# One transformer block with routed experts on one core: engine orders and PSUM homes rewritten, a payload ring of 8, loads and empty rows spread over the loop

## The chip, the cores and the metric

The kernel runs on 1 core of one Trainium2 chip. The metric is the device time in microseconds of one execution. Engines are TensorE (PE), VectorE (DVE), ScalarE (ACT), GpSimd (POOL) and SyncE (SP, which issues most of the DMAs here).

## What is computed

The input x has 4 batches of 1024 tokens of 128 numbers, float32. Six vectors per batch come from a small matrix on silu(c) and shift, scale and gate the two halves of the block:

```python
h = _layernorm(x) * (1 + ca) + sa
x = x + ga * attention(h)          # 16 query heads, 4 key heads, D = 64
h = _layernorm(x) * (1 + cb) + sb
x = x + gb * moe(h)                # 8 experts, 128 -> 512 -> 128, relu
```

The attention is causal with a window of 128 tokens, and its scores go through 30 * tanh(s / 30) before the softmax. The expert of a token is the argmax of its gate logits. An expert takes at most 512 tokens, in the order of the tokens; the output of a token is scaled by its gate, and a token that found no place gets nothing from the experts.

## The kernel before, in words

A tile is 128 tokens (32 tiles, 8 per batch); a block is two tiles (16 blocks). Each engine has one program, an order written out by hand: a Python loop over e in steps of two, in which each call names the tile that it works on relative to e. All waiting is by semaphores, and each engine and the SP queue take their instructions strictly in order.

**Per block.** DVE takes the statistics of x (`measure1`, `gather1`), POOL makes 1/std (`rstd1_of`), ACT normalises (`normalise1`), PE turns the tile (`turn_x`, L348), ACT writes the high part XH with scale and shift (`high_x`), and DVE writes the full value into the bank and the low part XL (`full_x`, `low_x`). Products of float32 are made from a high and a low part in three passes. PE projects k, v and four groups of q (`project_k` L356, `project_v` L367, `project_q` L380), and ACT copies each result out of its bank (`keep_k`, `keep_v`, `keep_q`).

**Per tile and half of the heads.** `score` (L391) writes the scores against the own tile to the fixed PSUM tile `own` and those against the tile before to `turns`; since `own` is one buffer, a score waits for the tanh of the one before. DVE merges both (`merge`, L865), ACT takes tanh and exp (`weigh` L689, `expose` L695), and POOL masks (`mask`, L1177). `sums` (L477) and `attend` (L456, L463) follow. A query reaches back into the tile before, and for the second half of the queries attend reads VM, whose first 64 rows are V of the tile and whose last 64 are V of the tile before. SP mixes it by two DMAs (`mix_v`, L286), after `v_kept`, and `VM` is a ring of 4. DVE divides by the sums (`turn_sums`, `invert`, `spread`, `scale` L896), ACT takes the high part OH (L701) and POOL the low part OL (`low_o`, L1185). `out_project` (L482) makes 24 matmuls per block, with OH and OL in turn.

**Then per tile.** ACT scales by ga (`keep_y`, L711), PE turns back (`turn_y`), DVE adds x (`add_x`, L907) and normalises again (`normalise2`, `modulate2`, `shift2`, the last of them frees the bank of `turn_y`), PE turns h (`turn_h2`) and scores the experts (`score_experts`), DVE finds the largest (`top8`, `which`), POOL marks it and counts (`mark`, `add_seen`), PE counts the places (`count`), DVE reads the place (`locate`), and POOL scatters the row PAY, which has h, the gate row, x and the token's number, to its place in `sorted_rows` in DRAM (`scatter`, L1221). SP also stores x to the output (`store_x`, L291). PAY is a ring of 4 rows of 400 numbers.

**Banks.** `turns` has six PSUM banks. The table HOME says which bank each use takes, and `take` waits for the engine that frees the bank's last use.

**Head.** SP loads x of batch 0, c, wmod, wk, wv, wq, the other three batches, wo, Wg and b1 (L253 to L263), then writes the empty rows for all 8 experts (L266, from the last row of PAY), then handles the small mod table, then w1 in one load of 2 MB (L276), and only then enters its loop with the `mix_v` of tile 1.

**Experts.** After the loop SP waits for all scatters and loads each expert's 512 rows and its w2 (L310 to L319). PE turns the rows (L596), makes the up and down products (L604, L617), ACT takes relu, DVE finishes, and POOL scatters to the output.

Of the kernel before, what the change touches and what calls it, by code (L numbers as in the profile page):

```python
# [37 lines left out]
ROW_H, ROW_G, ROW_X, ROW_ID, ROW = 0, P, 2 * P, 3 * P, 400  # L38
NO_TOKEN = 1 << 20

K_RING, Q_RING, V_RING, VD_RING, VM_RING, P_RING, PAY_RING = 3, 2, 6, 4, 4, 4, 4
# [5 lines left out]
    ("columns",): 0, ("rows",): 1,  # L47
    ("before", 0, 0): 2, ("before", 0, 1): 2, ("before", 1, 0): 2, ("before", 1, 1): 1,
    ("count", 0): 2, ("count", 1): 1,
    ("h2", 0): 4, ("h2", 1): 4,  # L50
    ("k",): 4,
    ("logits", 0): 4, ("logits", 1): 2,
    ("pv", 0): 4, ("pv", 1): 4,
    ("q", 0): 4, ("q", 1): 5, ("q", 2): 5, ("q", 3): 3,
    ("sums", 0): 5, ("sums", 1): 0,
    ("v",): 1,
    ("wo",): 1,
    ("x",): 1,
    ("y", 0): 1, ("y", 1): 0,
# [26 lines left out]
def build(nc, x, wq, wk, wv, wo, wg, w1, b1, w2, b2, c, wmod, out):  # L86
# [3 lines left out]
    with ctx:  # L90
# [28 lines left out]
        rows_at = sb("rows_at", [P, 2 * ST * ROW])  # L119
# [46 lines left out]
        empty_row = PAY[:, PAY_RING - 1, :]  # L166
# [3 lines left out]
        for wide in (rows_at[:, :], x_sb[:, :, :].rearrange("p a b -> p (a b)"),  # L170
                     Q[:, :, :, :].rearrange("p a b c -> p (a b c)"), PR[:, :, :].rearrange("p a b -> p (a b)")):
            for i in range(wide.shape[1] // (ST * ROW)):
                rows.append(wide[:, i * ST * ROW:(i + 1) * ST * ROW].rearrange("p (s r) -> p s r", r=ROW))
# [13 lines left out]

        x_in = [sem(f"x_in{b}") for b in range(BATCHES)]
        wk_in, wv_in, wq_in, c_in, wmod_in, wo_in, w1_in, b2_in, rest_in, mod_in = sems(
            "wk_in", "wv_in", "wq_in", "c_in", "wmod_in", "wo_in", "w1_in", "b2_in", "rest_in", "mod_in")  # L190
# [44 lines left out]
            (WkH[:, :], WkL[:, :], stage_k), (WqH[:, :QH], WqL[:, :QH], stage_q[:, :QH]), (WvH[:, :], WvL[:, :], stage_v),  # L235
            (WqH[:, QH:], WqL[:, QH:], stage_q[:, QH:]),
            (WoH[:, REP:, :], WoL[:, REP:, :], stage_o[:, REP:, :]), (WoH[:, :REP, :], WoL[:, :REP, :], stage_o[:, :REP, :]))
        SPLIT_K, SPLIT_Q0, SPLIT_V, SPLIT_Q1, SPLIT_O1, SPLIT_O0 = range(6)
        split_in = (wk_in, wq_in, wv_in, wq_in, wo_in, wo_in)
        CONSTS = 14  # L240
# [8 lines left out]
        def program_sp(sp):  # L249
# [3 lines left out]
            sp.dma_start(x_sb[:, 0:BATCH_TILES, :], x_v[0]).then_inc(x_in[0], 16)  # L253
            sp.dma_start(cT[:, :], c).then_inc(c_in, 16)
            sp.dma_start(stage_m, wmod).then_inc(wmod_in, 16)
            sp.dma_start(stage_k, wk).then_inc(wk_in, 16)
            sp.dma_start(stage_v, wv).then_inc(wv_in, 16)
            sp.dma_start(stage_q, wq).then_inc(wq_in, 16)
            for b in range(1, BATCHES):
                sp.dma_start(x_sb[:, b * BATCH_TILES:(b + 1) * BATCH_TILES, :], x_v[b]).then_inc(x_in[b], 16)  # L260
# [3 lines left out]
            sp.wait_ge(consts, CONSTS)  # L264
            for e in range(EXPERTS):
                sp.dma_start(sorted_v[e], empty_row.unsqueeze(1).to_broadcast([P, ST, ROW])).then_inc(empty_in, 16)  # L266
# [6 lines left out]
            sp.wait_ge(weights_l, len(split))  # L273
            sp.wait_ge(columns_done, 1)
            sp.wait_ge(rows_done, 1)
            sp.dma_start(w1_sb, w1.rearrange("e h f -> h e f")).then_inc(w1_in, 16)  # L276
# [16 lines left out]
            for e in range(-24, TILES - 14, 2):  # L293
                if is_tile(e + 23):
                    mix_v(e + 23)
                if is_tile(e + 14):
                    store_x(e + 14)
                if is_tile(e + 15):
                    store_x(e + 15)
                if is_tile(e + 24):  # L300
                    mix_v(e + 24)
# [21 lines left out]
        def program_pe(pe):  # L323
# [158 lines left out]
            def out_project(k):  # L482
                n, ps = take("wo", k)
                if k == 0:
                    pe.wait_ge(weights_l, SPLIT_O0 + 1)
                pe.wait_ge(ol_done, 4 * k + 4)
                y = ps[:, 0:BT]
                for i in range(2 * REP):
                    oh, ol = (o[:, :, :, i * HALF:(i + 1) * HALF] for o in (OH, OL))
                    pe.matmul(y, WoH[:, i, :], oh, start=(i == 0), stop=False)  # L490
                    pe.matmul(y, WoH[:, i, :], ol, start=False, stop=False)  # L491
                    last = pe.matmul(y, WoL[:, i, :], oh, start=False, stop=(i == 2 * REP - 1))  # L492
                last.then_inc(wo_done, 1)
                freed[n] = yT_kept, k + 1
# [37 lines left out]
            n, ps = take("rows")  # L532
            pe.matmul(ps[0:BATCHES, 0:3 * P], siluT[:, :], stage_m[:, 3 * P:6 * P], start=True, stop=True).then_inc(rows_done, 1)
# [5 lines left out]
            for e in range(-20, TILES - 8, 2):  # L539
                if is_tile(e + 10):  # L540
                    turn_h2(e + 10)
                if is_tile(e + 16):
                    project_q(e // 2 + 8, 1)
                    project_q(e // 2 + 8, 0)
                    project_q(e // 2 + 8, 3)
                if is_tile(e + 9):
                    count(e + 9)
                if is_tile(e + 14):
                    sums(e + 14)
                if is_tile(e + 10):  # L550
                    score_experts(e + 10)
                if is_tile(e + 15):
                    score(e + 15, 1)
                if is_tile(e + 14):
                    attend(e + 14)
                if is_tile(e + 16):
                    project_v(e // 2 + 8)
                    score(e + 16, 0)
                if is_tile(e + 12):
                    out_project(e // 2 + 6)  # L560
                if is_tile(e + 10):
                    count(e + 10)
                if is_tile(e + 11):
                    turn_h2(e + 11)
                if is_tile(e + 18):
                    project_q(e // 2 + 9, 2)
                if is_tile(e + 12):
                    turn_y(e + 12)
                if is_tile(e + 11):
                    score_experts(e + 11)  # L570
                if is_tile(e + 15):
                    sums(e + 15)
                if is_tile(e + 18):
                    project_k(e // 2 + 9)
                if is_tile(e + 16):
                    score(e + 16, 1)
                if is_tile(e + 15):
                    attend(e + 15)
                if is_tile(e + 20):
                    turn_x(e // 2 + 10)  # L580
                if is_tile(e + 17):
                    score(e + 17, 0)
                if is_tile(e + 13):
                    turn_y(e + 13)
# [47 lines left out]
        def program_act(act):  # L632
# [86 lines left out]
            def gate_row(t):  # L719
                act.wait_ge(gate_done, t + 1)  # L720
                if t == 0:
                    act.wait_ge(mod_in, 16)
                    act.wait_ge(empty_in, 16 * EXPERTS)
# [11 lines left out]

            act.wait_ge(c_in, 16)
            act.activation(c_e[:, :], cT[:, :], ACT.Exp, scale=-1.0).then_inc(c_exped, 1)
            split_high(SPLIT_K)
            split_high(SPLIT_Q0)
            split_high(SPLIT_V)  # L740
            split_high(SPLIT_Q1)
# [3 lines left out]
            for e in range(-18, TILES - 4, 2):  # L745
                if is_tile(e + 10):
                    expose(e + 10, 1)
                if is_tile(e + 9):
                    high_o(e + 9, 0)
                if is_tile(e + 6):  # L750
                    keep_h2(e + 6)
                if is_tile(e + 14):
                    high_x(e // 2 + 7)
                if is_tile(e + 12):
                    keep_q(e // 2 + 6, 1)
                if is_tile(e + 11):
                    weigh(e + 11, 0)
                if is_tile(e + 12):
                    keep_q(e // 2 + 6, 0)
                if is_tile(e + 11):  # L760
                    expose(e + 11, 0)
                if is_tile(e + 12):
                    keep_q(e // 2 + 6, 3)
                if is_tile(e + 9):
                    high_o(e + 9, 1)
                if is_tile(e + 11):
                    weigh(e + 11, 1)
                if is_tile(e + 5):
                    gate_row(e + 5)
                if e == -12:  # L770
                    split_high(SPLIT_O1)
                    split_high(SPLIT_O0)
                if is_tile(e + 12):
                    keep_v(e // 2 + 6)
                if is_tile(e + 6):
                    exp_gate(e + 6)
                if is_tile(e + 11):
                    expose(e + 11, 1)
# [531 lines left out]
```

## Time and profile before

| | |
|---|---|
| median of 3 runs | 476.62 us (475.41 to 477.88) |
| the profiled execution | 476.81 us, its span 475.1 us |
| mean granted clock of TensorE | 0.952 |
| busy: PE, POOL, ACT, DVE | 88%, 65%, 63%, 60% of the span |
| head, up to the first projection | 0 to 13.3 us |
| loop over the tiles | 13.3 to some 397 us |
| experts | 397 to 475 us |

A row of the timeline has the start and length in us, engine, line, operation, output <- inputs and count; what stands in brackets is the idle time before it and what ended it. A matmul's length includes its way through the array, so that those of one group overlap; the distance of two starts says more than the length. In the page and the windows "PEclk" is the granted clock as a share of full speed, where 0.50 is 1.2 GHz and 1.00 is 2.4 GHz.

### The profile page before, as it was taken

To read this page: it belongs to the slowest core of one execution; us is meant where nothing else is said; L and a number is where in the kernel's file an instruction comes from. 1 tells how busy PE (TensorE), PEld (TensorE's weight loads), DVE (VectorE), ACT (ScalarE), POOL (GpSimd) and SP (SyncE) were. 2 spreads that over 40 slices of the span, in tenths; PEclk is the share of its full clock that TensorE was granted. 3 is DMA by queue.
4 is the path that set the end of the run, shared out by engine and by line. 5 is a ranking of instruction groups with operands and counts; after the bars stand their busy time and mean duration, and the time that the engine had idled before them with its cause. 6 is when DMAs were issued, how large, how long until landed. Compare 5 with 4: busy or idle time off the path is not lost. (4 is left out here: it accounts for less than half of the span.)

```text
span 475.1 us, 14910 instructions
## 1 busy us (share of the span) xinstructions
PE 417.4 (88%) x5608; PEld 294.0 (62%) x5608; DVE 286.9 (60%) x846; ACT 298.0 (63%) x537; POOL 310.8 (65%) x494
## 2 busy tenths in 40 slices
PE   2894999999999999999999999999999742899970
PEld 1652566766767676666677666767565531799960
DVE  6263557775676868576777756675777541245631
ACT  4785457777776868777777778676756221564420
POOL 6136248587786969687867878676769851055572
PEclk9998899999999999999999999999999765999995
DMA  8987000101101010102011110101020125971110
GB/s 261 369 294 231 3 23 3 41 25 37 52 20 54 20 52 20 43 19 70 20 52 38 35 41 21 52 20 52 21 86 24 42 96 188 364 248 39 33 50 16
DMA packets 32078, 37.73 MB, mean 79 GB/s; under 512 B 3474, under 2 KB 28311, under 8 KB 32008
## 3 DMA queue, kind: packets, MB, share of 16 engines
q1 hardware_dynamic: 28936, 28.22, 19.1%
q0 software_dynamic: 3072, 8.56, 5.0%
q8 instruction: 46, 0.75, 0.6%
q14 instruction: 24, 0.20, 0.1%
HBM read 15.88 MB, written 17.31 MB: 70 GB/s over the span
## 5 line engine op out<-in xcount | busy, mean ns | idle before, releaser
L1185 POOL TENSOR_TENSOR OL<-O,OH 128x512 fp32r<-128x512 f32 x64 | 81.3, 1285 | 22.3 <-ACT OH L701 21.8
L865 DVE COPY_PREDICATED own<-before,turns 128x1024 f32<-128x1024 uint32 x56 | 68.8, 1229 | 40.3 <-PE turns L424 40.3
L689 ACT ACTIVATE PR<-own 128x1024 f32<-128x1024 f32 x64 | 65.5, 1024 | 42.4 <-DVE own L865 42.0
L1177 POOL TENSOR_SCALAR_AFFINE_SELECT PM<-PR 128x1024 f32<-128x1024 f32 x64 | 69.5, 1096 | 22.4 <-ACT PR L695 22.0
L695 ACT ACTIVATE PR<-PR 128x1024 f32<-128x1024 f32 x64 | 65.8, 1054 | 0.0
L420 PE MATMUL own<-Q,K 64*32 64x256 f32 (+3 forms) x896 | 58.8, 441 | 1.9 <-ACT PR L689 1.7
L896 DVE TENSOR_TENSOR O<-turns,R 128x512 f32<-128x512 f32 x64 | 41.2, 685 | 29.2 <-PE turns L463 28.9
L424 PE MATMUL turns<-Q,K 64*32 64x128 f32 (+3 forms) x896 | 57.4, 429 | 0.0
L701 ACT ACTIVATE OH<-O 128x512 fp32r<-128x512 f32 x64 | 40.0, 628 | 11.0 <-DVE O L896 10.9
L1221 POOL DMA_INDIRECT sorted_rows<-PAY,slot_i x32 | 35.1, 1096 | 14.0 <-issue 10.9
L424 PEld LDWEIGHTS turns<-Q,K 64*32 64x32 f32 x896 | 36.5, 107 | 9.4
L456 PE MATMUL turns<-PR,V 128*32 128x256 f32 x448 | 36.4, 394 | 6.1 <-DMA VM<-V 6.1
L344 PE MATMUL turns<-XH,WqH 128*128 128x256 f32 x128 | 39.2, 307 | 2.0 <-DVE XL L859 1.8
L675 ACT ACTIVATE Q<-turns 128x512 f32<-128x512 f32 x64 | 38.5, 601 | 4.0 <-PE turns L346 3.8
L490 PE MATMUL turns<-OH,WoH 128*128 128x256 f32 x128 | 38.4, 300 | 2.0 <-POOL OL L1185 2.0
L491 PE MATMUL turns<-OL,WoH 128*128 128x256 f32 x128 | 36.7, 287 | 0.0
L492 PE MATMUL turns<-OH,WoL 128*128 128x256 f32 x128 | 36.7, 286 | 0.0
L345 PE MATMUL turns<-XL,WqH 128*128 128x256 f32 x128 | 36.0, 281 | 0.0
L346 PE MATMUL turns<-XH,WqL 128*128 128x256 f32 x128 | 35.9, 280 | 0.0
L456 PE MATMUL turns<-PR,VM 128*32 128x256 f32 x448 | 35.8, 388 | 0.0
L463 PE MATMUL turns<-PM,VD 64*32 64x256 f32 x896 | 31.7, 391 | 0.0
L874 DVE STREAM_TRANSPOSE sumsT<-turns 128x512 f32<-128x512 f32 x32 | 22.9, 716 | 13.0 <-PE turns L477 12.2
(189 smaller groups left out, 1010.8 us busy)
## 6 DMA issues: line engine op xcount, KB each, us to landing
sorted_rows<-PAY SPq DMA_DIRECT2D x8, 800.0 KB, 12.1
VM<-V SPq DMA_DIRECT2D x56, 64.0 KB, 2.1
x_sb<-x_dram SPq DMA_DIRECT2D x4, 512.0 KB, 6.7
w_stage<-w_dram SPq DMA_DIRECT2D x1, 2048.0 KB, 10.9
out_dram<-PAY SPq DMA_DIRECT2D x32, 64.0 KB, 1.7
x_sb<-sorted_rows SPq DMA_DIRECT2D x2, 800.0 KB, 9.6
Q<-sorted_rows SPq DMA_DIRECT2D x2, 800.0 KB, 9.1
PR<-sorted_rows SPq DMA_DIRECT2D x2, 800.0 KB
```

The lines of the kernel that those rows point to most:

```text
L344: pe.matmul(dst, wh, xh, start=True, stop=False)
L420: pe.matmul(own[lo:lo + B, a, :].rearrange("p (r n) -> p r n", n=P)[:, :, lo:P], keys(a, t, lo, lo + B), q(a, lo, P), start=True, stop=Tru ...
L424: last = pe.matmul(ps[lo:lo + B, a, :].rearrange("p (r n) -> p r n", n=P)[:, :, 0:lo + B], keys(a, t - 1, lo, lo + B), q(a, 0, lo + B), st ...
L456: last = pe.matmul(out_of(c, x, g), v[:, d], probabilities(PM if first(t) else PR, slice(0, P), g, c), start=(x == 0), stop=(x == 1 and fi ...
L675: act.activation(Q[:, k % Q_RING, 2 * n:2 * n + 2, :], bank["q", k, n].rearrange("p (c n) -> p c n", c=2), ACT.Copy).then_inc(q_kept[n], 1)
L689: act.activation(pr, own[:, :, :].rearrange("p a n -> p (a n)"), ACT.Tanh, scale=SCORE_SCALE).then_inc(tanhed, 1)
L695: act.activation(pr, pr, ACT.Exp, scale=SOFTCAP).then_inc(exped, 1)
L701: act.activation(OH[:, t % 2, c, :], O[:, t % 2, c, :], ACT.Copy).then_inc(oh_done, 1)
L865: dve.copy_predicated(own[:, :, :].rearrange("p a (r n) -> p (a r) n", n=P), before[:, :].bitcast(U32).unsqueeze(1).to_broadcast([P, 2 * R ...
L896: dve.tensor_tensor(O[:, t % 2, c, :].rearrange("p (x r n) -> p x r n", x=2, n=HALF), bank["pv", t][:, c, :].rearrange("p (x r n) -> p x r ...
L1177: pool.affine_select(out=PM[:, u % P_RING, :].rearrange("p (r n) -> p r n", n=P), in_=PR[:, u % P_RING, :].rearrange("p (r n) -> p r n", n ...
L1185: pool.tensor_tensor(OL[:, t % 2, c, :], O[:, t % 2, c, :], OH[:, t % 2, c, :].bitcast(F32), ALU.subtract).then_inc(ol_done, 1)
```

## The change

- A row of PAY has 388 numbers instead of 400, in another order (h, number, gate, x), and PAY is a ring of 8. The empty row is a buffer of its own; scatter(0) alone waits for the empty rows, no longer `add_x`, `gate_row` and `name_row`.
- SP loads x of the first two tiles alone, then wk, wq in two parts, wv, the rest of batch 0, batch 1, wo, Wg, b1. ACT's queue loads c and wmod in two parts. The empty rows of two experts each stand behind the `mix_v` of tiles 1 to 4, batches 2 and 3 behind those of tiles 5 and 6, and w1 goes expert by expert behind later `store_x`.
- The splits into high and low parts have another order, and the copies for ga are made later (`keep_gate`).
- `out_project` makes the 16 matmuls with OH first, then waits for OL and makes its 8.
- All five engine orders and the table HOME are new. In PE's, V and one group of q are projected at the start of an iteration, before the attend of the tile two before them.
- The expert rows are read to other buffers (rows_at, Q, PR, x_sb, OH).

The orders of ACT, DVE and POOL are cut to the calls that matter below; the places of the others have moved too.

```diff
-K_RING, Q_RING, V_RING, VD_RING, VM_RING, P_RING, PAY_RING = 3, 2, 6, 4, 4, 4, 4
+K_RING, Q_RING, V_RING, VD_RING, VM_RING, P_RING, PAY_RING = 3, 2, 6, 4, 4, 4, 8
 HOME = {
...
+    ("before", 0, 0): 3, ("before", 0, 1): 1, ("before", 1, 0): 0, ("before", 1, 1): 3,
+    ("count", 0): 2, ("count", 1): 0,
+    ("h2", 0): 2, ("h2", 1): 1,
+    ("k",): 1,
+    ("logits", 0): 3, ("logits", 1): 2,
+    ("pv", 0): 1, ("pv", 1): 3,
+    ("q", 0): 3, ("q", 1): 5, ("q", 2): 5, ("q", 3): 2,
+    ("sums", 0): 1, ("sums", 1): 5,
+    ("v",): 4,
+    ("wo",): 4,
+    ("x",): 0,
+    ("y", 0): 0, ("y", 1): 5,
...
         def program_sp(sp):
+            sp.dma_start(x_sb[:, 0:2, :], x_v[0][:, 0:2, :]).then_inc(x_first, 16)
             sp.dma_start(stage_k, wk).then_inc(wk_in, 16)
+            sp.dma_start(stage_q[:, QH:], wq[:, QH:]).then_inc(wq1_in, 16)
+            sp.dma_start(stage_q[:, :QH], wq[:, :QH]).then_inc(wq0_in, 16)
             sp.dma_start(stage_v, wv).then_inc(wv_in, 16)
+            sp.dma_start(x_sb[:, 2:BATCH_TILES, :], x_v[0][:, 2:BATCH_TILES, :]).then_inc(x_in[0], 16)
+            sp.dma_start(x_sb[:, BATCH_TILES:2 * BATCH_TILES, :], x_v[1]).then_inc(x_in[1], 16)
...
-            for e in range(EXPERTS):
-                sp.dma_start(sorted_v[e], empty_row.unsqueeze(1).to_broadcast([P, ST, ROW])).then_inc(empty_in, 16)
...
-            sp.dma_start(w1_sb, w1.rearrange("e h f -> h e f")).then_inc(w1_in, 16)
...
+            for e in range(14, TILES + 22, 2):
+                if is_tile(e - 15):
+                    mix_v(e - 15)
+                if 1 <= e - 15 <= EXPERTS // 2:
+                    clear_rows(2 * (e - 15) - 2)
+                    clear_rows(2 * (e - 15) - 1)
+                if EXPERTS // 2 < e - 15 <= EXPERTS // 2 + 2:
+                    load_x(e - 15 - EXPERTS // 2 + 1)
+                if is_tile(e - 14):
+                    mix_v(e - 14)
+                if 1 <= e - 14 <= EXPERTS // 2:
+                    clear_rows(2 * (e - 14) - 2)
+                    clear_rows(2 * (e - 14) - 1)
...
+                if is_tile(e - 21):
+                    store_x(e - 21)
+                if is_tile(e - 20):
+                    store_x(e - 20)
+                if W1_TILE <= e - 22 < W1_TILE + 2 * EXPERTS:
+                    load_w1((e - 22 - W1_TILE) // 2)
...
             def out_project(k):
+                pe.wait_ge(oh_done, 4 * k + 4)
+                for i in range(2 * REP):
+                    oh = OH[:, :, :, i * HALF:(i + 1) * HALF]
+                    pe.matmul(y, WoH[:, i, :], oh, start=(i == 0), stop=False)
+                    pe.matmul(y, WoL[:, i, :], oh, start=False, stop=False)
                 pe.wait_ge(ol_done, 4 * k + 4)
                 for i in range(2 * REP):
+                    last = pe.matmul(y, WoH[:, i, :], OL[:, :, :, i * HALF:(i + 1) * HALF], start=False, stop=(i == 2 * REP - 1))
...
```

PE's new order in one iteration, each call under its own `is_tile`:

```python
for e in range(-16, TILES - 4, 2):
    project_v(e // 2 + 6); score_experts(e + 6); project_q(e // 2 + 6, 3); count(e + 5)
    sums(e + 10); turn_x(e // 2 + 8); score(e + 11, 1); attend(e + 10)
    out_project(e // 2 + 4); project_q(e // 2 + 7, 1); count(e + 6); turn_h2(e + 7)
    score(e + 12, 0); project_k(e // 2 + 7); turn_y(e + 8); score_experts(e + 7)
    sums(e + 11); project_q(e // 2 + 7, 0); score(e + 12, 1); attend(e + 11)
    project_q(e // 2 + 7, 2); score(e + 13, 0); turn_y(e + 9); turn_h2(e + 8)
```

Of DVE's (range(-8, TILES + 12, 2)), at e == 0 and then in each iteration:

```python
    measure1(e + 6)
    if e == 0: keep_columns(); split_low(SPLIT_K); split_low(SPLIT_Q1)
    full_x(e // 2); merge(e - 5, 1); spread(e - 6)
    if e == 6: split_low(SPLIT_O1); split_low(SPLIT_O0)
    ...
    merge(e - 4, 1); normalise2(e - 8); invert(e - 5); modulate2(e - 8); spread(e - 5)
    shift2(e - 8); scale(e - 5, 0); gather1(e + 7); scale(e - 5, 1); merge(e - 3, 0)
```

Of ACT's (range(-16, TILES - 2, 2)):

```python
    expose(e + 7, 1); keep_y(e // 2 + 2); keep_h2(e + 3); keep_q(e // 2 + 5, 1); gate_row(e + 2)
    keep_k(e // 2 + 5); weigh(e + 8, 0)
    ...
```

## Rows read from the trace of the kernel before

**Rows 1.** Page, part 1 (busy us, share, instructions); part 2, granted clock in 40 slices

```profile
PE 417.4 (88%) x5608; PEld 294.0 (62%) x5608; DVE 286.9 (60%) x846; ACT 298.0 (63%) x537; POOL 310.8 (65%) x494
...
PEclk9998899999999999999999999999999765999995
```

**Rows 2.** Windows: stretch, length, busy us by engine, granted clock, DMA share, GB/s

```profile
13.30:39.60 26.30, 24.74 (x280) 17.43 (x280) 11.45 (x24) 20.49 (x33) 8.41 (x15) 1.00 0.95 327
39.60:45.60 6.00, 0.00 (x0) 0.01 (x1) 2.47 (x5) 3.25 (x4) 5.01 (x5) 0.88 0.85 259
45.60:51.10 5.50, 5.48 (x65) 2.25 (x65) 0.00 (x0) 0.00 (x0) 0.21 (x1) 0.51 0.01 3
51.10:371.70 320.60, 316.32 (x4830) 212.86 (x4822) 224.05 (x661) 233.04 (x421) 240.35 (x380) 1.00 0.12 36
371.70:376.20 4.50, 1.12 (x9) 0.68 (x6) 2.71 (x13) 2.00 (x6) 4.50 (x7) 0.90 0.08 28
376.20:381.50 5.30, 5.26 (x24) 5.20 (x25) 1.00 (x3) 0.00 (x0) 2.83 (x9) 0.50 0.10 39
```

**Rows 3.** PE's waits, whole span: us in total, times, longest

```profile
PE turns L456 <- DMA VM<-V: 6.1, 1, 6.1
```

**Rows 4.** Timeline of the SP queue, 0 to 60 us: start, length, issues

```profile
10.76 11.56 SPq L266 DMA_DIRECT2D sorted_rows<-PAY  x8
...
34.20 0.38 SPq L276 DMA_DIRECT2D w_stage<-w_dram  x1
```

**Rows 5.** Page, part 6, whole span; last line: tile VM, 30 to 60 us

```profile
sorted_rows<-PAY SPq DMA_DIRECT2D x8, 800.0 KB, 12.1
...
VM<-V SPq DMA_DIRECT2D x56, 64.0 KB, 2.1
...
DMA to landing us min/median/max: 6.8/8.5/10.2
```

**Rows 6.** Timeline of PE: attend of a later tile, up to the next group

```profile
199.64 0.64 PE L456 MATMUL turns<-PR,V 128*32 128x256 f32 x8
...
202.53 0.44 PE L352 MATMUL turns<-ident,XN 128*128 128x128 f32 x2
```

**Rows 7.** Timeline of the head: first statistics, landing of wq, first projection

```profile
5.85 0.48 DVE L845 BATCH_NORM_STATS2 stats<-x_sb 128x6 f32<-128x128 f32 x2
...
8.07 0.63 ACT L635 ACTIVATE WqH<-w_stage 128x512 fp32r<-128x512 f32 x1 [1.28 <-DMA w_stage<-wq_dram]
...
13.30 0.55 PE L344 MATMUL turns<-XH,WqH 128*128 128x256 f32 x1 [1.83 <-DVE XL L859]
```

**Rows 8.** Timeline of PE: turn_x, one per block, of three blocks

```profile
51.08 0.44 PE L352 MATMUL turns<-ident,XN 128*128 128x128 f32 x2
...
72.26 0.44 PE L352 MATMUL turns<-ident,XN 128*128 128x128 f32 x2
...
312.49 0.44 PE L352 MATMUL turns<-ident,XN 128*128 128x128 f32 x2 [0.38 <-DVE PAY L933]
```

**Rows 9.** Page, part 5: the merge and the tanh between two scores

```profile
L865 DVE COPY_PREDICATED own<-before,turns 128x1024 f32<-128x1024 uint32 x56 | 68.8, 1229 | 40.3 <-PE turns L424 40.3
...
L689 ACT ACTIVATE PR<-own 128x1024 f32<-128x1024 f32 x64 | 65.5, 1024 | 42.4 <-DVE own L865 42.0
```

**Rows 10.** Timeline of PE: out_project at full clock, and what follows it

```profile
214.27 0.39 PE L490 MATMUL turns<-OH,WoH 128*128 128x256 f32 x1
...
217.12 0.18 PE L519 MATMUL turns<-onehot,earlier_b 128*128 128x8 bf16 x1
```

**Rows 11.** Timeline of the last block and its out_project

```profile
359.53 0.65 PE L420 MATMUL own<-Q,K 64*32 64x512 f32 x12 [0.67 <-ACT PR L689]
...
373.21 0.62 ACT L701 ACTIVATE OH<-O 128x512 fp32r<-128x512 f32 x1
...
373.62 2.47 POOL L1185 TENSOR_TENSOR OL<-O,OH 128x512 fp32r<-128x512 f32 x2
...
376.24 0.55 PE L490 MATMUL turns<-OH,WoH 128*128 128x256 f32 x1 [2.02 <-POOL OL L1185]
```

More of the change, by code:

```diff
@@ L46 @@
 HOME = {
[L47 to L59, printed above, removed]
+    ("columns",): 4, ("rows",): 2,
+    ("before", 0, 0): 3, ("before", 0, 1): 1, ("before", 1, 0): 0, ("before", 1, 1): 3,
[10 more added lines that the diff above has]
+    ("y", 0): 0, ("y", 1): 5,
 }
@@ L556, in program_pe @@
[L556 to L582, printed above, removed]
@@ L583, in program_pe @@
-                if is_tile(e + 13):
-                    turn_y(e + 13)
+                    turn_x(e // 2 + 8)
+                if is_tile(e + 11):
+                    score(e + 11, 1)
+                if is_tile(e + 10):
+                    attend(e + 10)
+                if is_tile(e + 8):
+                    out_project(e // 2 + 4)
+                if is_tile(e + 14):
+                    project_q(e // 2 + 7, 1)
+                if is_tile(e + 6):
+                    count(e + 6)
+                if is_tile(e + 7):
+                    turn_h2(e + 7)
@@ L587, in program_pe @@
+                if is_tile(e + 11):
+                    attend(e + 11)
+                if is_tile(e + 14):
+                    project_q(e // 2 + 7, 2)
+                if is_tile(e + 13):
+                    score(e + 13, 0)
+                if is_tile(e + 9):
+                    turn_y(e + 9)
+                if is_tile(e + 8):
+                    turn_h2(e + 8)
             for n in range(6):
@@ L841, in measure1 @@
             def measure1(t):
[L842 removed]
+                dve.wait_ge(x_first if t < 2 else x_in[t // BATCH_TILES], 16)
                 if t >= 2:
@@ L1048, in program_dve @@
[L1048 to L1057 removed]
+                if is_tile(e - 6):
+                    scale(e - 6, 0)
+                if is_tile(e - 9):
+                    modulate2(e - 9)
+                    shift2(e - 9)
@@ new lines, in program_dve @@
+                if is_tile(e - 8):
+                    normalise2(e - 8)
+                if is_tile(e - 5):
+                    invert(e - 5)
+                if is_tile(e - 8):
+                    modulate2(e - 8)
+                if is_tile(e - 5):
+                    spread(e - 5)
+                if is_tile(e - 8):
+                    shift2(e - 8)
+                if is_tile(e - 5):
+                    scale(e - 5, 0)
+                if is_tile(e + 7):
+                    gather1(e + 7)
```

472 lines of the change are left out of this document (236 added, 236 removed).

## The prediction

> **What bounds the kernel now.** The profiled execution took 476.81 us for a span of 475.1; the median of the three runs is 476.62, so the two can be used as one. All sums below are against 476.81. A measurement of this kernel can tell about 0.5% (2.4 us) from no change.
>
> I read the page first. PE is busy 88% and the next engine 65%, and the granted clock is below full in the slices around 48 us, from 368 to 416 us, and at the end [rows 1]. So I cut the span into windows at the places where PE stops [rows 2]. The long loop, 51.1 to 371.7, has 316.3 us of PE in 320.6. Its busy number is modelled, so I checked it by starts: turn_x runs once per block of two tiles, and from 51.08 to 312.49 it starts 13 times, 12 blocks of 21.78 us on average, the shortest 21.18 [rows 8]. A new order can win at most 12 x 0.60 = 7.2 us there. The losses of PE stand elsewhere. From 39.6 to 45.6 it does nothing, and then works until 51.1 at half clock (0.51) [rows 2]. The wait list names the cause: attend of tile 1 waits 6.1 us for the mixed V in VM [rows 3]. The SP timeline shows what these transfers stand behind: eight issues of empty rows from 10.76 that take 11.56 us, then the 2 MB of w1 at 34.20, and the VM transfers behind both [rows 4]. The first six take 6.8 to 10.2 us to land, where the median over the run is 2.1 [rows 5]. At the end, out_project of the last block waits until 376.24 for POOL's low parts and then runs at half clock until 381.5 [rows 2, 11].
>
> **The mixed V no longer waits (gain 8.6).** In the new SP program the VM transfers of tile 1 stand before any empty row, and w1 comes in eight pieces much later. V is also projected one block earlier against attend (project_v of tiles e+12, e+13 before attend of e+10), so the transfer has over a tile's time. The clears of two experts stand between the transfers of tiles 2 and 3: some 1.6 MB, which at 327 GB/s [rows 2] are 4.9 us, and tile 3's attend comes a tile later, half a block or 10.6 us [rows 8]. The 6.0 us of standstill go. The attend after it took 5.5 us; one at full clock takes 202.53 - 199.64 = 2.9 [rows 6], so the clock gives back 2.6. Sum 8.6. If the cover is gone (clears landing late), at most these 8.6 come back.
>
> **Head (gain 0).** x of tiles 0 and 1 comes alone and c and wmod go by ACT's queue. But DVE's new list has the statistics of tiles 2 to 6 before keep_columns, the splits and full_x(0), and those tiles sit behind x_first, wk, wq, wv. The bytes up to the end of batch 0 are the same 1.6 MB that had landed before when wq was there, at 8.07 [rows 7]. Behind it come three pairs of statistics at 0.5 to 0.7 each [rows 7], two splits, full_x and low_x, again near 13 us: first projection 13.2 against 13.30 [rows 7]. If DVE does not wait there, up to 2 us are won; if x arrives later, 1 is lost.
> A sentence on the queue by itself: the Trainium skill (DMA: Bandwidth & Descriptors, Issuing engines are not separate DMA queues) says that DMAs started by different engines share the same 16 DMA engines and only the issue time is saved. This speaks against a gain from ACT's queue and no run here shows it yet; the sum takes none either way.
>
> **Ramp (gain 0, from -3 to +2).** Before, 13.3 to 39.6 is 26.3 us with 24.7 of PE [rows 2]. The scores go one by one through own: a score needs the tanh of the one before, thus merge 1.23 and tanh 1.02 plus the latencies between [rows 9]. The new order does turn_x, q, k of the next block between them, also V and q3 of this one, but ACT has keep_k(1) before the first tanh, and DVE has the two splits of Wo (2 x 0.6) in the block of scores 1 and 2. I count three gaps of about 1 us for the new, for 1.6 us that the old one has idle and some that are hidden in its half-clock start. It is no row: I take 0 and keep both ends.
>
> **Loop (loss 1.5, from -5 to +1).** The same matmuls in another order; out_project has the same 24. All PSUM homes move. Two new meetings are tight: bank 4 holds y of out_project and the second half of the next score's before, with only q1, count and turn_h2 between; bank 0 is held by y of a tile until shift2, which DVE now does after merge 1.23, normalise2, invert, modulate2 and spread, while score(e+13, 0) wants bank 0 after attend 2.9 and q2. By durations the two come out within 0.5 us of each other. I put 0.1 us on each of 14 blocks. 0.35 each is the bad end; of the possible 7.2 gain I allow 1.
> The ring of 8 payloads removes waits of DVE and POOL only, which are not the bound: 0. The cover is PE's full loop. The rows of 388 numbers instead of 400 take 3% off transfers of the expert stage that run ahead of PE there: 0.
>
> **Last block (loss 1.3, from 0 to -2).** Before, the old order has out_project between score(30, 0) and score(30, 1). The new one has projections there, which do not exist for the last block; what is left is a turn_y, an expert score and sums, about 1.5 us, against merge and tanh with latencies, about 2.6. This costs 1.1, and the next score pair, which waits 0.67 now [rows 11], a little more.
>
> **Last out_project (gain 3.5, from 2.5 to 4.9).** It used to start when OL was there (373.62 + 2.47 = 376.09, start 376.24). Sixteen of its 24 matmuls now need OH alone, done at 373.83 [rows 11]. At full clock 24 take 2.85 us (217.12 - 214.27) [rows 10], so 16 from 373.9 end at 375.8, and 8 with OL, ready at about 375.7, end at 376.7. Against 381.5 this gives 4.8. If the clock is half from the start, as it was at 376.2 [rows 2], 16 take 3.5 and 8 take 1.8: 379.2, gain 2.3. The clock was still 0.90 over 371.7 to 376.2, so it lies between; I take 3.5. What comes behind it (YT, the norms, routing, the scatter, the load of rows) is the same chain and moves with it.
>
> **Sum.** 8.6 + 0 + 0 - 1.5 - 1.3 + 3.5 = 9.3 us, 476.81 - 9.3 = 467.5.
>
> **Rivals.**
> A. The forecast, 467.5: chance 0.61.
> B. The loop has room. For it: the loop's weight loads are busy 212.9 of 320.6 us, 66% [rows 2]. Against: blocks already repeat within 0.6 us of the shortest. If the new order took 5 of the 7.2 us instead of losing 1.5, the time is 461.0. Chance 0.14. By the Trainium skill (Trainium Kernel Development and Optimization, Best Practices) matmul busy time misleads and LDWEIGHTS busy share tells the distance to the roofline; by that rule there is a third of the loop free, and B would be too small. The trace speaks against it: the spacing of the 24 matmuls at full clock is 0.119 us each, without a wait.
> C. The stall moves. A mixed V of tile 3 or 5 lands behind the clears beside it, or the ramp loses what the stall had hidden: PE waits, and the clock falls again. Price: the 8.6 gone, thus 476.1. For it: VM landings of up to 10.2 us behind other transfers [rows 5]. Against: over a tile of slack. Chance 0.13.
> D. Slower. DVE's shift2 comes too late for score(e+13, 0) by bank 0 in every block. One us per block over 14 blocks, instead of 1.5 in all, makes 467.5 + 12.5 = 480.0. Without its 1.5 the loop would leave 466.0, so it passes the old time from 0.76 us per block (466.0 + 10.6). For it: merge and the five operations behind it fill the gap to within 0.5 us. Against: DVE is busy 224 of 320.6 us. Chance 0.12.
>
> **Numbers.** Bounds of A: best 476.81 - (8.6 + 2 + 2 + 1 + 4.9) = 458.3, worst 476.81 - (8.6 - 1 - 3 - 5 - 2 + 2.5) = 476.7; all ends together are unlikely. 461 to 474.5 leaves out half of C, most of D and little of A and B, together under 0.2. Faster by over 0.5% (below 474.2): A 0.59, B 0.14, C 0.05, D 0.04, sum 0.82. Within 0.5%: A 0.02, C 0.06, D 0.02, sum 0.10. Slower: C 0.02, D 0.06, sum 0.08.
>
> **What would show it.** No wait of PE for VM, and no half clock before 60 us, shows the first step. The first projection near 13 and the first turn_x after attend(1) some 8 us earlier show head and ramp. The distance of turn_x over twelve blocks shows the loop: 261 to 263 for A, under 257 for B, over 268 for D, with the wait named at scores or project_v. OH matmuls at least 2 us before the last OL end shows the last step. It would be wrong if VM waits return, if the loop grows, or if PE's pause in the last block is longer than 3 us.

## The result and the profile after

The changed kernel takes 465.13 us (median of 4, 464.12 to 465.36) against 476.09 for the kernel before beside it: ratio 0.976, 95% interval 0.9728 to 0.9792, 11.0 us. Measured again later beside the kernel before, it gave 465.17 and 0.9764 (0.9734 to 0.9794). The forecast was 467.5 in a range of 461 to 474.5. The profiled execution took 464.12 us, 12.7 less than that of before; 1.4 of these belong to the last stretch, from the last down product to the end, which took 16.4 us in this trace, 17.8 before and 18.0 in the second trace of the changed kernel.

The page after, busy time and granted clock, answers to [rows 1]:

```profile
PE 413.0 (89%) x5608; PEld 291.8 (63%) x5608; DVE 285.5 (62%) x846; ACT 299.7 (65%) x537; POOL 309.5 (67%) x495
...
PEclk9999999999999999999999999999999955999996
```

The dip of the clock in the fourth and fifth slices is gone. The windows of the changed kernel (stretch, length, busy us by engine PE, PEld, DVE, ACT, POOL, then granted clock, DMA share, GB/s), cut at the first projection, the end of attend(1), the end of the last attend, and around the last out_project, answer to [rows 2]:

```profile
14.10:44.83 30.73, 29.04 (x352) 20.46 (x351) 16.60 (x42) 24.66 (x39) 12.70 (x21) 1.00 0.57 196
44.83:362.80 317.97, 314.94 (x4821) 211.77 (x4813) 221.56 (x658) 233.43 (x419) 241.14 (x379) 1.00 0.17 50
362.80:365.70 2.90, 0.91 (x15) 0.59 (x7) 2.05 (x7) 1.67 (x4) 2.65 (x4) 1.00 0.18 69
365.70:369.30 3.60, 3.11 (x24) 2.92 (x25) 1.23 (x9) 1.06 (x4) 3.34 (x8) 1.00 0.06 18
```

The 6 us without PE and the attend at half clock have no counterpart. The last out_project runs at full clock in this trace. In the second trace of the same kernel it does not: there the window around it has

```profile
364.20:368.80 4.60, 4.60 (x27) 4.56 (x27) 1.51 (x9) 0.61 (x3) 3.89 (x9) 0.63 0.05 14
```

The waits of PE in the changed kernel, first trace, answer to [rows 3]:

```profile
PE turns L375 <- ACT XN L671: 5.5, 1, 5.5
...
PE turns L544 <- POOL onehot L1237: 3.8, 3, 2.1
PE turns L530 <- DVE PAY L965: 3.2, 3, 2.5
...
PE own L443 <- ACT PR L718: 2.0, 3, 1.4
```

No wait for VM is left. On the SP queue of the changed kernel (start, length, issue), the VM transfers stand ahead of the empty rows, as against [rows 4]:

```profile
22.13 1.17 SPq L297 DMA_DIRECT2D VM<-V  x2
23.35 1.16 SPq L279 DMA_DIRECT2D sorted_rows<-empty_row  x2
...
30.72 1.11 SPq L297 DMA_DIRECT2D VM<-V  x2
31.87 1.17 SPq L279 DMA_DIRECT2D sorted_rows<-empty_row  x2
33.08 2.63 SPq L297 DMA_DIRECT2D VM<-V  x2
```

By the view of tile VM from 15 to 60 us they land in 1.9 to 5.9 us, where it was 6.8 to 10.2 [rows 5]:

```profile
DMA to landing us min/median/max: 1.9/2.0/5.9
```

**Where the time went.** I put the traces side by side at places where PE has done the same work. The second trace of the changed kernel was taken later; its time, 465.33 us, is the nearer to the median.

| place | before | after | second trace after | lead of after | lead of second |
|---|---|---|---|---|---|
| first projection | 13.30 | 14.10 | 13.68 | -0.8 | -0.4 |
| end of attend(1), 1.3 us of work (a turn_x, a group of q) more done in after | 51.08 | 44.83 | 43.35 | 7.5 | 9.0 |
| end of the last attend | 371.68 | 362.82 | 361.33 | 8.9 | 10.3 |
| YT of the last block | 381.74 | 368.84 | 368.84 | 12.9 | 12.9 |
| first rows of the experts turned | 400.13 | 388.30 | 387.57 | 11.8 | 12.6 |
| start of the last down product | 457.23 | 445.87 | 445.62 | 11.4 | 11.6 |
| end of the span | 475.1 | 462.3 | 463.6 | 12.8 | 11.5 |

### The profile page after: what moved, and what is told of

Read it like the earlier page. It is cut to its first block and busy times, and to the rows that moved or that the text cites. A ratio compares the mean times of both kernels' runs of the same rounds, so it can differ in the third digit from the quotient of the medians.

```text
span 462.3 us, 14917 instructions
## 1 busy us (share of the span) xinstructions
PE 413.0 (89%) x5608; PEld 291.8 (63%) x5608; DVE 285.5 (62%) x846; ACT 299.7 (65%) x537; POOL 309.5 (67%) x495
## 5 line engine op out<-in xcount | busy, mean ns | idle before, releaser
L724 ACT ACTIVATE PR<-PR 128x1024 f32<-128x1024 f32 x64 | 67.1, 1048 | 0.1
L443 PE MATMUL own<-Q,K 64*32 64x128 f32 (+3 forms) x896 | 58.7, 441 | 2.5 <-ACT PR L718 2.0
L930 DVE TENSOR_TENSOR O<-turns,R 128x512 f32<-128x512 f32 x64 | 43.0, 682 | 17.2 <-PE turns L486 17.0
L1262 POOL DMA_INDIRECT sorted_rows<-PAY,slot_i x32 | 34.7, 1085 | 12.3 <-issue 11.5
L447 PEld LDWEIGHTS turns<-Q,K 64*32 64x32 f32 x896 | 36.6, 107 | 9.5
L367 PE MATMUL turns<-XH,WqH 128*128 128x256 f32 x128 | 41.1, 321 | 0.0
L367 PEld LDWEIGHTS turns<-XH,WqH 128*128 128x128 f32 x128 | 25.0, 195 | 18.7 <-issue 9.5
L479 PE MATMUL turns<-PR,V 128*32 128x256 f32 x448 | 35.1, 385 | 0.0
L479 PE MATMUL turns<-PR,VM 128*32 128x256 f32 x448 | 34.4, 379 | 0.0
L513 PE MATMUL turns<-OH,WoH 128*128 128x256 f32 x128 | 32.7, 294 | 0.9 <-ACT OH L730 0.9
L1231 POOL TENSOR_SCALAR var<-mv 128x1 f32<-128x1 f32 x32 | 6.2, 192 | 38.8 <-DVE mv L949 37.5
L514 PE MATMUL turns<-OH,WoL 128*128 128x256 f32 x128 | 31.0, 281 | 0.0
```

The lines of the kernel that those rows point to most:

```text
L367: pe.matmul(dst, wh, xh, start=True, stop=False)
L443: pe.matmul(own[lo:lo + B, a, :].rearrange("p (r n) -> p r n", n=P)[:, :, lo:P], keys(a, t, lo, lo + B), q(a, lo, P), start=True, stop=Tru ...
L447: last = pe.matmul(ps[lo:lo + B, a, :].rearrange("p (r n) -> p r n", n=P)[:, :, 0:lo + B], keys(a, t - 1, lo, lo + B), q(a, 0, lo + B), st ...
L479: last = pe.matmul(out_of(c, x, g), v[:, d], probabilities(PM if first(t) else PR, slice(0, P), g, c), start=(x == 0), stop=(x == 1 and fi ...
L724: act.activation(pr, pr, ACT.Exp, scale=SOFTCAP).then_inc(exped, 1)
L930: dve.tensor_tensor(O[:, t % 2, c, :].rearrange("p (x r n) -> p x r n", x=2, n=HALF), bank["pv", t][:, c, :].rearrange("p (x r n) -> p x r ...
```

## The experiments

**1. Which load made the stall: w1 alone.** The prediction blamed both the empty rows and w1. The first edit moves only w1 in the kernel before, with the three waits ahead of it, one of them for the splits of Wo:

```diff
-            sp.dma_start(w1_sb, w1.rearrange("e h f -> h e f")).then_inc(w1_in, 16)
+                if e + 14 == 8:
...
+                    sp.dma_start(w1_sb, w1.rearrange("e h f -> h e f")).then_inc(w1_in, 16)
```

> The kernel before, with one edit: the 2 MB load of w1 moves from ahead of the first mixed V to behind the store of tile 9. Theory (the stall is the w1 load): the first VM transfers are issued at 33.3 instead of 34.63 and have only the 768 KB mod load ahead, land by 38.5, before attend of tile 1 is ready at 39.5; the 6.0 us of standstill and the 2.6 us of half clock go, 476.1 - 8.6 = 467.5. Rival (the empty rows are the cause, since SP reaches its loop only at 32.9 behind them): VM still lands late, gain under 3 us, 473 or more.

Measured: 469.08 us against 475.87, ratio 0.9848 (0.9829 to 0.9868), a gain of 6.8. The timeline and, in the last line, the view of tile VM up to 60 us:

```profile
33.00 0.35 SPq L271 DMA_DIRECT2D mod<-mod_dram  x1
33.40 2.70 SPq L281 DMA_DIRECT2D VM<-V  x3
...
43.53 0.44 PE L352 MATMUL turns<-ident,XN 128*128 128x128 f32 x2
...
DMA to landing us min/median/max: 1.9/2.2/4.0
```

VM is issued hardly earlier (33.4 instead of 34.6), but it lands in 4.0 us at most, and turn_x of block 3, at 51.08 before, comes at 43.53. The rival falls. The gain is 1.8 short of the forecast. Some 1.0 of it is there at turn_x of block 3, since attend(1) is not ready at 39.5 here but starts at 40.64, of which 0.6 us is a later first projection (13.89). The lead is still 7.7 when the first rows of the experts are turned (392.39 against 400.13), and 6.5 at the start of the last down product; why 1.2 us go there stays open.

**2. The empty rows alone.**

```diff
-            for e in range(EXPERTS):
-                sp.dma_start(sorted_v[e], empty_row.unsqueeze(1).to_broadcast([P, ST, ROW])).then_inc(empty_in, 16)
...
+                if 1 <= t <= EXPERTS // 2:
+                    for e in (2 * t - 2, 2 * t - 1):
+                        sp.dma_start(sorted_v[e], empty_row[:, :].unsqueeze(1).to_broadcast([P, ST, ROW])).then_inc(empty_in, 16)
```

> The kernel before, with the empty rows of two experts each behind the mixed V of tiles 1 to 4 (an empty row buffer of its own, scatter(0) alone waits for them), w1 still in one load ahead of the loop. Theory: SP waits there for the splits of Wo, which DVE ends at 34.2, so w1 and the VM transfers behind it start no earlier than before, and the stall stays: 474 to 477. Rival (empty rows are the cause): 467.5.

Measured: 475.01, ratio 0.9973 (0.9957 to 0.9988), 0.9 us. PE's wait list first, then the SP timeline, of this kernel:

```profile
PE turns L462 <- DMA VM<-V: 5.0, 1, 5.0
```

```profile
15.08 0.35 SPq L268 DMA_DIRECT2D mod<-mod_dram  x1
35.19 0.38 SPq L273 DMA_DIRECT2D w_stage<-w_dram  x1
35.61 0.60 SPq L283 DMA_DIRECT2D VM<-V  x1
```

SP issues nothing from 15.4 to 35.2: it stands at its wait for the last split of Wo, which DVE ends at 35.16, and the VM transfers stand behind that wait and behind 2 MB. The stall stays, as expected. In the kernel before the same wait held SP for 0.9 us only (the mod table's load was issued at 32.93, behind the empty rows, and w1 at 34.20). So either of the two, the empty rows or the wait, puts w1 at this time, and this run alone does not say that the empty rows were harmless; run 1 does, where they and the mod table stay in front.

**3. Both.** The two edits together.

> The kernel before, with both edits: empty rows behind the mixed V of tiles 1 to 4 and w1 behind the store of tile 9. Theory: the stall goes as with w1 alone, 467.5, at most 1 us from that run. Rival (each of the two carries a part): at least 3 us below the better of the two single edits.

Measured: 468.33, ratio 0.9833 (0.9815 to 0.9852). That is 7.5 us of gain, 0.75 below w1 alone, with overlapping intervals. The VM transfers of tile 1 are issued at 23.0 now, ten us earlier than in run 1, and it hardly matters. The loads account for 7.5 of the 11.0 us, almost all by w1.

**4. The old SP order in the changed kernel.** Empty rows and w1 ahead of the loop again:

```diff
+            for e in range(EXPERTS):
+                sp.dma_start(sorted_v[e], empty_row[:, :].unsqueeze(1).to_broadcast([P, ST, ROW])).then_inc(empty_in, 16)
...
+            sp.dma_start(w1_sb, w1.rearrange("e h f -> h e f")).then_inc(w1_in, 16)
```

> The changed kernel, with empty rows and w1 put back ahead of SP's loop, all else as changed. Theory: w1 is issued near 34.5 again and VM of tile 1 lands near 45, where attend of tile 1 is ready at 41.9: 3 to 4 us of standstill and 1 to 2.6 us of half clock, 465.1 + 5 = 470. Rival (the new order needs the early VM more, tiles 2 and 3 wait too): over 473. Rival (the new order would have hidden it anyway): 465 to 466.

Measured: 472.64 (470.08 to 474.8), ratio 0.9932 (0.9907 to 0.9958). PE's wait list and the SP timeline:

```profile
PE turns L466 <- DMA VM<-V: 4.5, 1, 4.5
```

```profile
35.59 0.38 SPq L282 DMA_DIRECT2D w_stage<-w_dram  x1
36.01 3.94 SPq L292 DMA_DIRECT2D VM<-V  x6
```

The stall is back at the same place, with VM issued within 1.4 us of the old time. The profiled execution, 470.08, is the theory's 470; the median is 2.6 above, and its executions scatter more than those of the other kernels. By the ratios the old SP order costs 8.2 us here (0.9932 against 0.976). The rival that the new order hides the stall is out. The rival of over 473 is not: three of the seven executions took 473.5 to 474.8, and what makes them slower stays open, since only the fastest was profiled.

**5. The old out_project in the changed kernel.**

```diff
+                pe.wait_ge(ol_done, 4 * k + 4)
...
-                pe.wait_ge(oh_done, 4 * k + 4)
...
-                    pe.matmul(y, WoL[:, i, :], oh, start=False, stop=False)
-                pe.wait_ge(ol_done, 4 * k + 4)
...
+                    pe.matmul(y, WoH[:, i, :], ol, start=False, stop=False)
+                    last = pe.matmul(y, WoL[:, i, :], oh, start=False, stop=(i == 2 * REP - 1))
```

> The changed kernel, with the old out_project (OH and OL passes in turn, one wait for OL ahead). Theory: the last one starts when OL is there, 1.9 us later (367.6 instead of 365.7) or more, and perhaps at half clock, which costs 2 to 4 us; the other 15 give back 0.10 us each (2.85 us in the trace before, 2.95 after), 1.5 us. Net 465.1 + 1.5, between 465.5 and 468. Rival (OL is ready in time in the new order anyway): 463.6, since only the 1.5 us remain.

Measured: 467.0 against 465.13 to 465.17 of the changed kernel, ratio 0.981 (0.9791 to 0.983). Its last out_project in the timeline:

```profile
366.64 0.55 PE L513 MATMUL turns<-OH,WoH 128*128 128x256 f32 x1 [2.88 <-POOL OL L1224]
...
371.04 0.47 ACT L738 ACTIVATE YT<-turns,ga_col 128x256 f32<-128x256 f32 x1 [5.56 <-PE turns L515]
```

It waits 2.88 us for OL, and its first matmul has the length of half clock (0.55); the mean granted clock of the product, 366.64 to 371.01, is 0.68. The kernel of run 6 differs from this one in block 15 alone and took 464.54 beside it, so the split in the last block is worth 2.5 us.

**6. Is the new pass order dearer per block?** Out_project takes 2.94 to 2.96 us per block in the trace after and 2.84 to 2.94 before. I held the pass order responsible and kept it for block 15 alone:

```diff
+                if k == BLOCKS - 1:
+                    ...
+                else:
+                    ...
```

> The changed kernel, with the old out_project in blocks 0 to 14 and the new one in block 15 alone. Theory (the new pass order costs 0.10 us per block by its matmuls): 465.1 - 1.5 = 463.6. Rival (the 0.10 us lies in how the trace counts a group's end, or is taken back at the next group): 465.1.

Measured: 464.54, ratio 0.9754 (0.9735 to 0.9773), 0.6 us below the changed kernel, within its interval and between the two expectations, so the time decides nothing. The trace does: blocks 0 to 14 still take 2.94 to 2.96 us, with the old pass order. The 0.1 us is not the pass order; I was wrong. What else in the new order makes it was not tried.

**7. The new out_project alone, in the kernel before.** The edit is the one of the change.

> The kernel before, with the new out_project alone. Theory: in the last block 16 matmuls run before OL is there and the clock stays up, 3.3 us gained, less 15 times 0.10: 476.1 - 1.8 = 474.3. Rival (the clock falls there anyway): 476.1 - 2.3 + 1.5 = 475.3. Rival (a part of the changed loop's gain comes from it): below 473.

Measured: 474.16 against 476.35, ratio 0.9951 (0.9934 to 0.9968), a gain of 2.2. The theory said 474.3, but with a cost of 1.5 us in the loop that does not exist (blocks of 2.83 to 2.94 us here, as before); the agreement is luck, and the gain at the end is smaller than the 3.3 that it took. In this trace the way from the last attend to YT is 7.1 us instead of 10.1. The timeline shows why it is not shorter:

```profile
373.72 0.28 PE L491 MATMUL turns<-OH,WoL 128*128 128x256 f32 x1
373.83 0.28 PE L490 MATMUL turns<-OH,WoH 128*128 128x256 f32 x1
373.94 0.34 PE L491 MATMUL turns<-OH,WoL 128*128 128x256 f32 x1
374.08 0.42 PE L490 MATMUL turns<-OH,WoH 128*128 128x256 f32 x1
374.30 0.42 PE L491 MATMUL turns<-OH,WoL 128*128 128x256 f32 x1
```

The distance of two starts grows from 0.11 to 0.22 us in the middle of the product: the clock had stayed up through the start and fell to half during it. In the first trace of the changed kernel it stayed at 1.00 to the end, in the second it fell after six matmuls, at 365.0.

**8. The ring of 8.**

```diff
-K_RING, Q_RING, V_RING, VD_RING, VM_RING, P_RING, PAY_RING = 3, 2, 6, 4, 4, 4, 8
+K_RING, Q_RING, V_RING, VD_RING, VM_RING, P_RING, PAY_RING = 3, 2, 6, 4, 4, 4, 4
```

> The changed kernel with a payload ring of 4 instead of 8. Theory (the ring takes away only waits of engines with slack): 465.1, within 1 us. Rival (the new SP order stores x of tile t only after the mixed V of tile t + 6 or t + 7, so DVE's add_x waits and holds the merge behind it): 2 us or more slower, with PE waits at scores.

Measured: 464.34, ratio 0.9752 (0.9732 to 0.9772). The ring of 8 brings nothing, as the prediction had it, and the blocks of this trace repeat as those of the changed kernel do.

**9. A better head.** DVE of the changed kernel stands still until x of tiles 2 to 7 is there, with the work of tile 0 behind it. The edit puts that work first:

```diff
+                if e == -4:
+                    keep_columns(); split_low(SPLIT_K); split_low(SPLIT_Q1); full_x(0); low_x(0)
+                if e == -2:
+                    split_low(SPLIT_Q0); split_low(SPLIT_V)
...
-                if is_tile(e + 16):
+                if is_tile(e + 16) and e != -14:
                     turn_x(e // 2 + 8)
...
                     project_q(e // 2 + 7, 0)
+                if e == -14:
+                    turn_x(1)
```

> The changed kernel with DVE's head in another order: keep_columns, splits of K and Q1, full_x(0), low_x(0) stand before the statistics of tiles 2 and 3, the splits of Q0 and V before those of 4 and 5; turn_x(1) goes behind the projection of q group 0. Theory (the head waits for x of tiles 2 to 7, which lands at 9.25): the first projection starts near 10 instead of 14.1, and of the 4 us some 2 to 4 reach the end: 461 to 463. Rival (ACT and DVE chains of the ramp decide, not PE's start): the scores come as late as before, 464.5 to 465.5.

Measured: 461.36, but beside a kernel before that took 471.17 on that chip, ratio 0.9804 (0.9788 to 0.982). The absolute time looks like a success, and the ratio, 9.8 us of gain where the changed kernel had 11.0, says that there is none. The head did move, by its timeline:

```profile
11.25 0.58 PE L367 MATMUL turns<-XH,WqH 128*128 128x256 f32 x1 [2.89 <-DVE WqL L875]
...
15.09 0.38 PE L375 MATMUL turns<-ident,XN 128*128 128x128 f32 x2
```

The first projection comes at 11.25, not near 10, since it now waits for the split of q. From there to turn_x of block 4 it is 36.6 us, and 35.5 and 34.4 in the two traces of the changed kernel: the chain of scores, tanh and merge in the ramp takes part or all of the gain back.

**10. Head and last block together,** then both kernels once more on one chip.

> Both: the head as above, and the new out_project in block 15 alone. Theory: the two gains add, 1.5 us below the head alone. Rival: within 0.5 us of the head alone.

Measured: 460.65, ratio 0.9775 (0.9761 to 0.979), 0.7 below the head alone. That lies between theory and rival and decides nothing.

> The changed kernel again, beside the next. Theory: the same ratio to the kernel before as the first time, 0.976, whatever chip it falls on. The stretch from the last down product's start to the end, 16.4 us in its first trace and 17.7 to 17.9 in those of seven other kernels, is 17.7 or so again if it is a matter of the execution, 16.4 if it is one of this kernel.

Measured: 465.17, ratio 0.9764 (0.9734 to 0.9794). First projection 13.68, turn_x of block 4 at 48.08. The last stretch took 18.0 us, so the 16.4 of the first trace was a matter of the execution. So was more: turn_x of block 4 came at 49.57 there, and the last out_project ran at full clock there and fell to half clock here.

> The changed kernel with DVE's new head and the new out_project in the last block alone. Theory (half a microsecond from each): 0.5 to 1.5 us below the changed kernel on the same chip. Rival (the ramp takes the head's gain back): within 0.5 us of it.

Measured: 465.37, ratio 0.9775 (0.9746 to 0.9803), beside 465.17 for the changed kernel. First projection 11.24, but turn_x of block 4 at 48.24: the 2.4 us are gone within the ramp. The rival holds, and no version here beats the changed kernel by more than the measurement can tell.

## Why the prediction was right

**Mixed V, forecast 8.6.** Right in kind: no wait for VM, no half clock. The lead after attend(1) is 7.5 in the first trace, which is 8.6 less 0.8 of the head and 0.3 of the ramp, and 9.0 in the second. The runs that isolate the loads give 7.5 (run 3) and 8.2 (run 4). Wrong in the weight of the causes: the prediction put the empty rows beside w1, and alone they are worth 0.9 us (run 2) against 6.8 for w1 (run 1). What cost the time was the 2 MB load directly in front of the VM transfers. In run 1 SP comes to them hardly earlier, still behind the empty rows, and the stall is gone. The wait for the splits of Wo kept the load at that place when the empty rows were out of the way (run 2); a kernel without that wait and with the load in front was not tried.

**Head, forecast 0.** It is 0.8 late in the first trace and 0.4 in the second. The step that was off is the landing of x for tiles 2 to 7, put at some 8 us by counting bytes. The timeline after, up to the first projection:

```profile
9.25 0.49 DVE L879 BATCH_NORM_STATS2 stats<-x_sb 128x6 f32<-128x128 f32 x2 [4.31 <-DMA x_sb<-x_dram]
...
13.78 0.66 PE L375 MATMUL turns<-ident,XN 128*128 128x128 f32 x2 [5.45 <-ACT XN L671]
14.10 0.56 PE L367 MATMUL turns<-XH,WqH 128*128 128x256 f32 x1
```

Directly in front of the projection PE waited for XN, with turn_x of the second block in its order ahead of it; the low part XL was done at 12.87. The prediction did not have this wait.

The trace does not contradict the Trainium skill (DMA: Bandwidth & Descriptors, Issuing engines are not separate DMA queues): with c and wmod on ACT's queue the loads as a whole ended no sooner. Of wmod, now in two parts, the first had landed at 4.8 us and the second at 6.0, where the whole had landed at 6.0 before; x of the batch was there later.

**Ramp, forecast 0.** -0.3 in the first trace and +0.8 in the second, both inside its bounds. The two differ in how long PE's matmuls start at half the pace, 0.21 us apart: until 19.6 in the first trace and until 16.6 in the second. The granted clock reads 1.00 in this stretch of both, so it does not show this, and why the pace is half there stays open. Run 9 and the last run show that the ramp is a chain of its own, on which an earlier start is mostly lost.

**Loop, forecast a loss of 1.5.** This term had the wrong sign and came out above its best end, a gain of 1. The lead grows by 1.3 between attend(1) and the last attend in both traces, with a loss of 0.7 in the last block in between, so the loop gained about 2. PE's turn_x in the trace after:

```profile
49.57 0.44 PE L375 MATMUL turns<-ident,XN 128*128 128x128 f32 x2
...
71.24 0.44 PE L375 MATMUL turns<-ident,XN 128*128 128x128 f32 x2
...
287.96 0.44 PE L375 MATMUL turns<-ident,XN 128*128 128x128 f32 x2
```

Eleven blocks take 238.39 us, 21.67 each; the same eleven, from 72.26 to 312.49 [rows 8], took 240.23 before. All nine traces with the new order have 238.4, whatever else was changed in them, and the five with the old order have 239.4 to 240.2. So the gain belongs to the new order, and neither the new out_project (run 7) nor the ring (run 8) makes it; which part of the order does was not tried. The shortest block is 20.98 now, below the 21.18 from which the prediction took its largest gain. The tight meetings at banks 4 and 0 that I priced at 0.1 us a block produce one wait of 0.44 us in the whole loop, near its end (at 338.50, for YT). Rival D had the one at bank 0 as its mechanism and is out.

Of rival B the size is out, 5 us of gain in the loop and 461.0 in all, but its direction was the right one: the measured 2 lies between its 5 and the forecast's -1.5, and twelve blocks at 21.67 are 260, below the 261 to 263 that stood for A and above the 257 that stood for B. The weight loads are busy for 211.8 of 318.0 us, 67%, as before 66%. By the Trainium skill (Trainium Kernel Development and Optimization, Best Practices), which judges the distance to the roofline by MFU and the busy share of the weight loads, that share would still leave a third of the loop. No run here shows whether it is free. The prediction's 0.119 us per matmul against it is from out_project alone, where the weight loads are busy for 2.92 of PE's 3.11 us (window 365.70 above), and says nothing on the rest of the loop. What the trace shows is that PE has no wait above 0.25 us from attend(1) to 338 us, so that whatever is left lies in the matmuls and weight loads themselves or in waits shorter than that.

**Last block, forecast a loss of 1.3.** The pause is where it was put and of its size, in the timeline after:

```profile
342.60 0.65 PE L443 MATMUL own<-Q,K 64*32 64x512 f32 x12 [1.41 <-ACT PR L718]
```

Before it was 0.67 one score later [rows 11], so the net loss is about 0.7.

**Last out_project, forecast 3.5.** From the end of the last attend to YT it took 10.1 us before. It took 6.0 in the first trace, 4.0 gained, and 7.5 in the second, 2.5 gained. The timeline of the first:

```profile
364.31 1.23 ACT L730 ACTIVATE OH<-O 128x512 fp32r<-128x512 f32 x2 [0.38 <-DVE O L930]
365.02 2.52 POOL L1226 TENSOR_TENSOR OL<-O,OH 128x512 fp32r<-128x512 f32 x2 [0.20 <-ACT OH L730]
...
365.68 0.36 PE L513 MATMUL turns<-OH,WoH 128*128 128x256 f32 x1 [0.92 <-ACT OH L730]
```

The matmuls with OH start 1.9 us ahead of the last OL (367.54), a little short of the 2 us that the prediction asked for. The full clock to the end was luck: the 24 matmuls take 3.1 us at 1.00 here and 4.6 at 0.63 in the second trace, and the prediction was right to put its 3.5 between a full and a half clock. The runs that isolate the split give 2.5 (run 5 against run 6) and 2.2 us (run 7). With the old pass order in the changed kernel (run 5) the way from the last attend to YT is 9.2 us, so the new orders of DVE, ACT and POOL bring at most 0.9.

**Behind it, forecast 0.** "The same chain and moves with it" was not quite so: from YT to the first rows of the experts it took 18.4 us before, 19.5 in the first trace and 18.7 in the second. In the first trace PE waits three times for POOL's mark ahead of `count`, 3.8 us in all. Two of these waits, 1.2 and 2.1 us, are in the second trace too, and the kernel before has two at the same product of 1.2 and 2.0, put down to other things. The third, 0.5 us right behind out_project, is in the first trace alone; what makes the rest of the 1.1 stays open. So part of what a full clock wins in out_project is lost behind it: from the last attend to the first rows it is 28.5 us before and 25.5 and 26.2 after.

**The sum** was 9.3 and the medians give 11.0. The second trace leads by 11.5 at its end, 2.2 more than the sum: the loop 3.5 more than forecast, the ramp 0.8 and the last block 0.6 more, the last out_project 1.0 less, the head 0.4 less, and from YT to the last down product another 1.3 that the forecast had at 0. The range was met with the largest term right and several small ones wrong in both directions, which cancelled in part; that much of the closeness is luck.

## What to carry to other kernels

Look at what a queue's first small transfer stands behind, and ask of each item what it makes that transfer wait for: one load of 2 MB directly in front of it cost 6.8 us of a 476 us kernel, while the 6 MB of empty rows that stood out in the profile cost under 1. A wait further up can be what keeps such a load in its place. Where a product has parts that are ready at different times, do the ready ones first, above all where the engine would otherwise stand idle and lose its clock. An earlier start is only worth what the chain behind it lets through. A version from another chip is compared by its ratio and not by its time, and a stretch of one trace is checked in a second trace of the same kernel before it is put down to the change.

## What the runs showed of the hardware

The clock in the last out_project is not a property of the kernel. Of the eight traces in which the changed order has the ready matmuls first, three ran all 24 at 1.00 (3.1 us, and 3.5 in run 9, which waited within it for OL) and five at a mean of 0.63 to 0.67 (4.3 to 4.6 us). Both traces of the changed kernel have the same 318.0 us between attend(1) and the last attend and the same granted clock of 1.00 in the 3 us before the product. What decides it stays open.

The end of the kernel differs between chips. From the start of the last down product to the end of the span, eleven of the fourteen traces took 17.7 to 18.0 us, whatever the kernel; the first trace of the changed kernel 16.4; and both traces on the chip where the kernel before takes 471.2 us 14.6. The kernel with the new head and the new out_project in block 15 ran on that chip and on another: 14.6 us and 460.65 in all on the one, 18.0 and 465.37 on the other. The place is DVE's wait ahead of the last pair of tiles. Two timeline rows show it, first of the kernel before, then of run 9:

```profile
465.14 0.42 DVE L1110 TENSOR_TENSOR R<-turns,V 128x256 f32<-128x256 f32 x1 [4.40 <-remote]
```

```profile
447.99 0.42 DVE L1155 TENSOR_TENSOR R<-turns,V 128x256 f32<-128x256 f32 x1 [0.44 <-PE turns L648]
```

One waits 4.40 us for something that the profile does not name, the other 0.44 for PE. What it is stays open; the shorter stretch is 3 of the 5 us by which that chip is faster.
